# Transformer block on one core: low part of the maxima on GpSimd, high part by a one-tensor maximum, all lists reordered

## What is computed

```python
x = x + layernorm(attention(layernorm(x)))      # 16 heads of 8, 4 key/value heads, causal
x = x + layernorm(ffn(layernorm(x)))            # one 128x128 matmul

# attention
qkv = x @ W_qkv + b_qkv
scores = where(causal, q @ k.T / sqrt(8), -inf)
y = softmax(scores) @ v
return y @ W_out + b_out

# ffn
w = ternary_quantize(weight) * alpha
return x @ w.T + bias
```

## Time and profile before

| | |
|---|---|
| median of 3 runs | 456.02 us (455.45 to 457.24) |
| the profiled execution's own time | 456.64 us |
| its span, first to last instruction | 454.8 us |
| mean granted clock of TensorE | 0.97 |
| PE busy | 398.6 us, 88% |
| DVE busy | 394.7 us, 87% |
| ACT busy | 333.3 us, 73% |
| POOL busy | 296.3 us, 65% |
| DMA, share of 16 engines on SP's queue | 41.7% |

### The profile page before, as it was taken

One profiled execution on the slowest core, in us unless ns is written; L12 is line 12 of the kernel. 1 busy time (PEld: TensorE's weight loads), 2 busy tenths in 40 slices (PEclk: granted clock), 3 DMA queues, 4 the chain that ended last, 5 costly groups with the idle time before them and its releaser, 6 DMA issues.

```text
span 454.8 us, 19223 instructions
## 1 busy us (share of the span) xinstructions
PE 398.6 (88%) x7430; PEld 280.8 (62%) x7430; DVE 394.7 (87%) x1180; ACT 333.3 (73%) x609; POOL 296.3 (65%) x552
## 2 busy tenths in 40 slices
PE   0569999999999999999999999999999999998551
PEld 0336766676666676666666666676676777764330
DVE  5957878999999999999999999999999989995442
ACT  0333877777888888888888888888888888888332
POOL 2622323657677877777777777787777666766676
PEclk9999999999999999999999999999999999999855
DMA  7176465524434344444344444443444543421342
GB/s 190 35 121 94 103 107 133 127 75 85 77 72 80 81 76 81 78 76 79 66 70 77 76 72 80 81 75 80 82 74 85 114 84 69 87 77 30 111 145 73
DMA packets 72307, 39.59 MB, mean 87 GB/s; under 512 B 13048, under 2 KB 68056, under 8 KB 72216
## 3 DMA queue, kind: packets, MB, share of 16 engines
q1 hardware_dynamic: 70880, 37.70, 41.7%
q10 hardware_dynamic: 1336, 0.66, 0.5%
HBM read 13.67 MB, written 4.72 MB: 40 GB/s over the span
## 4 chain that ended last, share of the span: by engine, by line
PE 47%; DVE 29%; issue 9%; DMA 4%; POOL 3%; SPq 3%; ACT 2%; POOLq 0%; DVEq 0%; ACTq 0%
DVE M L619 13%; PE ps_mx L843 13%; PE ps_y L816 11%; PE ps_w L872 7%; PE ps_st L792 7%; PE ps_w L913 5%; DVE stats L584 4%; DVE xn L602 3%; DMA QS<-part 3%; DVE A L666 2%; DVE mv L594 2%; PE ps_w L893 2%; DVE Mp L683 2%; DVE F L674 2%; SPq L260 2%
## 5 line engine op out<-in xcount | busy, mean ns | idle before, releaser
L619 DVE TENSOR_REDUCE M<-ps_mx 128x2 f32<-128x512 f32 (+3 forms) x352 | 210.5, 626 | 14.2 <-PE ps_mx L843 13.5
L419 ACT ACTIVATE PT<-ps_st 128x1024 f32<-128x1024 f32 (+1 forms) x192 | 165.3, 884 | 20.4 <-PE ps_st L792 20.3
L843 PE MATMUL ps_mx<-KS,QS 112*64 112x128 bf16 (+2 forms) x2560 | 132.7, 228 | 15.9 <-DVE M L619 11.6
L843 PEld LDWEIGHTS ps_mx<-KS,QS 112*64 112x64 bf16 x2560 | 89.6, 112 | 60.9 <-DVE M L619 37.2
L358 POOL TENSOR_TENSOR rstd<-vareps,mhalf 128x2 f32<-128x2 f32 x128 | 93.0, 727 | 10.0
L792 PE MATMUL ps_st<-QS,KS 114*64 114x256 bf16 (+1 forms) x1024 | 97.9, 300 | 0.2 <-DMA QS<-MpT 0.2
L816 PE MATMUL ps_y<-PT,VB 128*32 128x256 f32 (+3 forms) x2048 | 90.4, 304 | 1.3 <-ACT PT L419 1.0
L356 POOL TENSOR_TENSOR vareps<-mv,eps 128x2 f32<-128x2 f32 x128 | 25.9, 203 | 73.3 <-DVE mv L594 73.3
L816 PEld LDWEIGHTS ps_y<-PT,VB 128*32 128x32 f32 x2048 | 46.7, 109 | 28.6 <-issue 9.4
L393 POOL TENSOR_TENSOR rest<-QK,part 128x512 f32<-128x512 f32 x32 | 38.2, 1193 | 24.3 <-ACT part L448 24.1
L792 PEld LDWEIGHTS ps_st<-QS,KS 114*64 114x64 bf16 x1024 | 52.0, 111 | 1.5 <-DMA QS<-MpT 0.5
(11 more groups left out here) (63 smaller groups left out, 512.9 us busy)
## 6 DMA issues: line engine op xcount, KB each, us to landing
QS<-part SPq DMA_DIRECT2D x192, 64.0 KB
rden<-rec_dram SPq DMA_DIRECT2D x32, 256.0 KB
X<-in_x SPq DMA_DIRECT2D x7, 512.0 KB, 6.3
out<-X SPq DMA_DIRECT2D x7, 512.0 KB, 5.4
KS<-part SPq DMA_DIRECT2D x32, 96.0 KB
KS<-part SPq DMA_DIRECT2D x32, 64.0 KB
KS<-part SPq DMA_DIRECT2D x32, 32.0 KB
QS<-MpT SPq DMA_DIRECT2D x32, 16.0 KB
```

The lines of the kernel that those rows point to most:

```text
L419: nc.scalar.activation(PT[(b * CHUNKS + n) % TILES][:, 0:512 * banks], ps_st[n % 2][:, 0:banks, :].rearrange("p a c -> p (a c)"), ACT.Exp, ...
L619: nc.vector.tensor_reduce(M[b % 2][:].rearrange("p k g i -> p (k g) i")[:, 2 * kv:2 * kv + pairs, i], ps_mx[(b * BANKS + n) % 2][:, 0:pair ...
L843: last = pe.matmul(ps_mx[(b * BANKS + n) % 2][64 * one:64 * one + 64, at:at + w], q[:, h, BL * i:BL * i + BL], k[:, kv, blocks, :], start= ...
```

## The change

The high part of the maxima is made by a `tensor_reduce` over an axis of length 1, and the low part on POOL (`low_max`), which waits for it. The orders of all five lists change: of SP, POOL, ACT, DVE and PE. DVE does all of batch 0's maxima before its steps and begins them at t = 6 in place of 7; they end at B + 12. PE does the turn and projection of batch 1 ahead of its steps.

```diff
@@ SP
             def step(t):
                 load_x(t)
+                k_rows(t - 1, 1)
+                send_den(t - 4)
+                k_rows(t - 1, 2)
                 rows_free(t)
+                q_rows(t, 0, 4)
+                store_rec(t - 4)
+                store_x(t - 27)
...
                 k_rows(t, 0)
...
+                spread_rec(t - 4)
                 send_max(t - 2)
@@ POOL
+            def low_max(b):
+                if on(b):
+
+                    gp.wait_ge(s_mp, 2 * b + 1)
+                    gp.tensor_tensor(Mp[:, 1, :], M[b % 2][:].rearrange("p k g i -> p (k g i)"), Mp[:, 0, :],
+                                     ALU.subtract).then_inc(s_mp, 1)
+
             def step(t):
-                add_normed(t - 10, A2, s_a2, s_x1)
-                third(t - 4)
-                inverse(t, 0)
-                divide(t - 9)
-                inverse(t - 10, 2)
-                inverse(t - 12, 3)
-                inverse(t - 9, 1)
                 remainder(t - 3)
                 add_normed(t - 13, F2, s_f2, s_fin)
+                low_max(t - 5)
+                inverse(t - 9, 2)
+                third(t - 3)
+                inverse(t - 8, 1)
+                inverse(t - 11, 3)
+                add_normed(t - 8, A2, s_a2, s_x1)
+                inverse(t, 0)
+                divide(t - 7)
@@ ACT
             def step(t):
+                take_qk(t - 1)
+                take_y(t - 5)
+                exp(t - 4, 0)
+                exp(t - 4, 1)
+                take_xn3(t - 8)
+                first_part(t - 1)
+                exp(t - 4, 2)
                 take_v(t - 1)
                 exp(t - 4, 3)
+                second_part(t - 1)
+                norm(t - 10, 3, F1, F2, s_f2, s_fin)
                 take_turned(t - 3)
+                exp(t - 4, 4)
                 take_xn1(t)
-                exp(t - 4, 4)
                 exp(t - 4, 5)
...
                 norm(t - 6, 1, A1, A2, s_a2, s_x1)
...
@@ DVE
-            def split_max(b):
-                if on(b):
-                    m = M[b % 2][:].rearrange("p k g i -> p (k g i)")
+            def high_max(b):
+                if on(b):
 
                     dve.wait_ge(s_mx, BANKS * b + BANKS)
                     free(dve, b, s_mt_ps)
-                    nc.vector.tensor_tensor(Mp[:, 0, :], m, m, ALU.max).then_inc(s_mp, 1)
-                    dve.wait_ge(s_mp, 2 * b + 1)
-                    nc.vector.tensor_tensor(Mp[:, 1, :], m, Mp[:, 0, :], ALU.subtract).then_inc(s_mp, 1)
+                    nc.vector.tensor_reduce(Mp[:, 0, :], M[b % 2][:].rearrange("p k g i -> p (k g i)").unsqueeze(2), AX_X,
+                                            ALU.max).then_inc(s_mp, 1)
@@ PE
             def step(t):
-                st(t - 4, 4)
+                pv(t - 4, 1)
+                pv(t - 4, 2)
+                pv(t - 4, 3)
                 x1(t)
...
```

More of the change, by code:

```diff
@@ L316, in step @@
                 load_x(t)
+                k_rows(t - 1, 1)
+                send_den(t - 4)
+                k_rows(t - 1, 2)
                 rows_free(t)
+                q_rows(t, 0, 4)
+                store_rec(t - 4)
+                store_x(t - 27)
+                q_rows(t, 0, 2)
+                q_rows(t, 0, 3)
                 k_rows(t, 0)
[L319 to L322, removed]
+                spread_rec(t - 4)
                 send_max(t - 2)
+                q_rows(t, 1, 5)
                 q_rows(t, 1, 1)
[L325 to L328, removed]
                 q_rows(t, 2, 0)
-                spread_rec(t - 4)
-                send_den(t - 3)
-            for t in range(B + 25):
+            for t in range(B + 27):
                 step(t)
@@ L695, in step @@
             def step(t):
[L696 to L712, removed]
+                spread_f(t - 12)
+                high_max(t - 6)
+                take_a(t - 9)
                 moments(t - 1, 0)
+                spread_a(t - 9)
                 spread_x(t)
[L715 to L718, removed]
+                moments(t - 9, 1)
+                moments(t - 12, 3)
+                maxima(t - 5, 0)
+                maxima(t - 5, 1)
                 norm_x(t - 2)
-                maxima(t - 6, 3)
+                maxima(t - 5, 2)
+                norm_x1(t - 10)
+                maxima(t - 5, 3)
+                maxima(t - 5, 4)
+                maxima(t - 5, 5)
+                maxima(t - 5, 6)
+                take_f(t - 11)
+                spread_x1(t - 9)
+                maxima(t - 5, 7)
+                moments(t - 9, 2)
+                maxima(t - 5, 8)
+                invert_den(t - 7)
+                maxima(t - 5, 9)
+                maxima(t - 5, 10)
             spread_x(0)
@@ L724, in _ @@
             masks()
-            fill(0)
             spread_x(1)
@@ L729, in _ @@
             norm_x(0)
+            fill(0)
             moments(2, 0)
@@ L733, in _ @@
             norm_x(1)
+            constants()
             moments(3, 0)
+            fill(2)
             spread_x(4)
-            constants()
             norm_x(2)
-            fill(2)
+            ternary()
             moments(4, 0)
-            ternary()
+            fill(3)
             spread_x(5)
[L742 to L745, removed]
             maxima(0, 0)
             maxima(0, 1)
+            norm_x(3)
             maxima(0, 2)
-            norm_x(4)
             maxima(0, 3)
-            for t in range(7, B + 14):
+            maxima(0, 4)
+            maxima(0, 5)
+            maxima(0, 6)
+            maxima(0, 7)
+            maxima(0, 8)
+            maxima(0, 9)
+            maxima(0, 10)
+            for t in range(6, B + 12):
                 step(t)
@@ L961, in _ @@
             v(0)
+            x1(1)
+            qk(1)
             constants()
-            for t in range(1, B + 8):
+            v(1)
+            mx(0, 0)
+            mx(0, 1)
+            for t in range(2, B + 8):
                 step(t)
```

35 lines of the change are left out of this document (12 added, 23 removed).

## The result

The changed kernel takes 489.3 us (488.13 to 492.27, 4 runs) against 456.12 for the kernel before in the same comparison: a ratio of 1.073, with a 95% interval of 1.069 to 1.076. It is **7% slower**. I had forecast 434 us.

What follows compares the result with a forecast made beforehand. It took DVE as the fuller engine, in a 12.36 us loop with PE. 27 steps falling to 11.7 us give 17.8, the end 4.5: 22.3 us off 456.64, so 434 us, range 423 to 451.

Steps and rivals of the forecast that it cites:

- the paragraph on SP: SP's DMA list: K rows a step later, maxima sent behind the Q rows and the broadcast of the reciprocals; cost 0.
- DVE's total: DVE's work per step: 12.36 less 1.03 plus 0.2, and without two waits 11.0 us, the floor of a step.
- PE's half: PE's stretch of the new loop, from maxima bank 2 to the output projection: 21 pieces, 8.83 us.
- The end: After the last high part: batch 28's A comes sooner, the 8.0 us chain stays; gain 4.5 us, between 1.5 and 6.
- The start: Before the steps: masks filled later, batch 1 projected before PE's constants; 0, within 1.5 us either way.
- The slower one: Rival: ACT's exponential ahead of its xn1T copy delays PE's q and k projection; up to 462 us, chance 0.11.
- The port takes it back: Rival: stalls behind POOL move to other DVE operations, above all the xn pairs, returning 0.83 us a step; 452 us, chance 0.05.
- DVE as the bound of the old step: In the kernel before, DVE is the fuller engine and PE follows; the loop of 12.36 us has 6.67 on DVE.
- 27 full steps: Mid-run of the kernel before: 27 steps counted at the full 12.36 us, each falling to 11.7, 17.8 us in all.

Runs made afterwards that it cites:

- the quarter of the broadcast: The changed kernel with the broadcast of the reciprocals moving a quarter of its columns, 64 KB in place of 256 KB (wrong numbers in the rest): 449.5 us, ratio 0.984.
- the kernel with the split alone: The kernel before with only the high part as TENSOR_REDUCE on DVE and the low part on POOL, every list as before: 457.81 us, ratio 1.002.

## Why the prediction was wrong, point by point

**The step that failed** is the paragraph on SP: "Cost 0: bank 0 stands at the end of PE's step and scores 0 more than a third into the next, over 4 us after the turn. Without that cover each 0.1 us of delay costs 2.7 us in all." The distance was right: the turn ended at 253.7 and PE stood ready at 258.1. But I never set a transfer's time against it. The copy takes 0.56 us, the wait behind the broadcast's issue some 0.5, and the transfer 5.2. In the step shown 1.9 us were missing. The mean step that I forecast was 11.97 - 17.8 / 31 = 11.40 us, and it is 13.10: 31 x 1.7 = 53 of the 55 us by which I was off. Of these, 38 us lie in the last 27 steps (12.88 us where the forecast comes to 12.15 - 17.8 / 27 = 11.49), and the quarter of the broadcast takes them off but for 1 us (11.54). The other 15 us lie in the first four steps, which I had left as they were. There the quarter helps by only 3 us; the chain shows the K rows, which the same paragraph puts a step later without a price, and the granted clock is 0.81 in place of 1.00. No run tells how much of the 15 us is the K rows' and how much the new lists of the engines'. The way of the denominators I did not price at all, though it is the same kind of step, and it is the one that keeps the fault alive when SP's order is mended.

**What I could have read.** The profile of before has hardly a wait for these transfers from 100 to 400 us, and I took that as a sign that they cost nothing. It says only that 5.3 and 8.9 us were enough. The distance in the old lists is what a new order has to be held against. There was also a duration: in the fill of the kernel before, PE's loads stand 0.45 us for the maxima at 65.40, and the chain of that stretch shows the transfer.

```profile
61.27 4.09 DMA QS<-MpT
```

With the copy of 0.57 us ahead of it that is 4.7 us, against a distance of "over 4 us".

**DVE's total: right.** The high part takes 0.168 us in the median (I took 0.2), the low part 0.244 on POOL. DVE is busy for 80.0 of 100 us at 13.2 us a step, so 10.6 us a step, where I had 11.0. The two pairs of xn and the run from A to bank 0 in the changed kernel:

```profile
252.17 0.17 DVE L690 TENSOR_REDUCE Mp<-M 128x32 bf16<-128x32 f32 x1
252.51 0.42 DVE L674 TENSOR_TENSOR A<-ps_w,bo_sb 128x256 f32<-128x256 f32 x1 [0.17 <-PE ps_w L882]
...
254.04 1.26 DVE L627 TENSOR_REDUCE M<-ps_mx 128x2 f32<-128x512 f32 x2
255.22 0.59 DVE L610 TENSOR_SCALAR xn<-X,mv,rstd 128x128 f32<-128x128 f32 x2
...
256.19 0.59 DVE L610 TENSOR_SCALAR xn<-X,mv,rstd 128x128 f32<-128x128 f32 x2
```

Both pairs take 0.59: no stall. From A (252.51) to the end of bank 0 are 2.2 us where I had 2.73. The small reduce takes 0.166 to 0.186 us in all 32 steps; the one at 252.17 runs beside POOL's addition of 251.60 to 252.33. This agrees with what the page "SBUF — State Buffer" of the Trainium skill ("Who interferes with whom") says of tensor_reduce, that it never contends on trn2.

The low part, which I cost at nothing, is not quite free: PE's loads at the turn wait for it 6.6 us from 100 to 400 us, in 12 steps.

**PE's half: right.** From bank 2 (255.07) to the end of the output projection (267.14) are 12.07 us; less the 1.94 of standing and the 1.6 of the clock it is 8.5, and I had 8.83. With a quarter of the broadcast the last 27 steps take 11.54 us each, so the new lists of the engines can run at the 11.7 that I forecast. It was the right bound of engines, and the wrong bound of the kernel.

**The end: right.** The A of batch 28 comes at 444.55, 0.1 us after the last high part, and three more follow at 8.3 us each:

```profile
444.55 0.42 DVE L674 TENSOR_TENSOR A<-ps_w,bo_sb 128x256 f32<-128x256 f32 x1
...
469.54 0.42 DVE L674 TENSOR_TENSOR A<-ps_w,bo_sb 128x256 f32<-128x256 f32 x1 [2.72 <-PE ps_w L882]
```

The gain is 4.3 us where I had 4.5, in part by luck: seen from the last high part the first A came 5.5 us sooner where I had 4.5, and the three behind it lost 0.9 (8.3 us each in place of 8.0). The start is 1.0 later, within my 1.5.

**The rivals.** The slower one, which I gave 0.11, had the wrong mechanism: ACT is not late with xn1T in the changed kernel. "The port takes it back" does not happen there, but in the kernel with the split alone it is what happens, 0.77 of 0.83 us; I had given it 0.05. A rival on transfers was missing.

**DVE as the bound of the old step: half right.** The chain ran through DVE, but PE was close behind. With 1.17 us a step taken off DVE, the step fell from 12.36 to 11.74 and PE stopped it. The count of 27 full steps was too high as well: only 18 steps of the kernel before have the full 12.35 us (129.29 to 351.67), and the last 27 have a mean of 12.15.

## What to carry to other kernels

When a hand-written order is changed, list for each transfer the time from its issue to the first instruction that needs it, before and after, in steps as well as in microseconds. A way of several transfers in a row needs its whole length, and a pipeline that is cut by half a step may bind though no wait showed it before. Look at the first steps by themselves: here they hold 15 of the 35 us that the steps lost.

If an operation is moved off a full engine, look at what it stood in front of: the entries behind it arrive earlier and can meet another engine's work at a shared port. Here moving one pair by three entries made the difference between 0 and 3%.

## What the runs showed of the hardware

- A transfer of 16 KB took 4.1 to 6.0 us (maxima) and 3.0 to 5.4 us (den) where it stood in the chain of the changed kernel, at a mean DMA share of only 0.4. With a quarter of the broadcast den took 3.6 us in the median in place of 4.6. A queue of its own did not help (6.1 us in the median on ACT's). 192 KB less a batch took 40 us off the kernel that was short of time for it, and nothing off the other.
- A stand of PE of 1.94 us, which ended at 260.08, was followed by pieces of twice their duration, 1.6 us lost on top of the stand. The length of the stand alone does not decide it: the granted clock was 0.50 from 224 to 226 us after one of 2.87 us that ended at 221.30, and stayed at 1.00 after those of 2.20 us that ended at 169.46 and of 2.04 us that ended at 275.05.
- A pair of TENSOR_SCALARs (128x128, float32) takes 0.59 us alone, and 0.94 or 1.71 us beside a POOL multiplication of 1.27 us, by when it starts. In both cases one of the two instructions ends 0.08 us after POOL's does (269.60 against 269.52, 221.61 against 221.53): it stands until POOL is done. The page "SBUF — State Buffer" of the Trainium skill ("Who interferes with whom") describes this lock, and says that whoever issues first gets the port. The order of the starts in the trace does not tell who that is: at 220.16 DVE's instruction starts 0.09 us ahead of POOL's, and is the one that stands.
